# Eighteen more indirect transfers in the preparation of a four-layer graph network kernel

## The reference, cut to what matters

```python
edge_index = jnp.stack([src, dst])
x = _layernorm(x + _L0_gnn_ref(x, edge_index, ...), axis=-1)   # two GATv2 passes
x = _layernorm(x + _L1_gnn_ref(x, edge_index, ...), axis=-1)   # roles of source and target exchanged
x = _layernorm(x + _L2_gnn_ref(x, ..., edge_index), axis=-1)
x = _layernorm(x + _L3_gnn_ref(x, edge_index, ...), axis=-1)   # eight heads
```

## Time and profile before

| | us |
|---|---|
| median of 3 runs | 12944.22 |
| lowest and highest run | 12932.75 and 12955.25 |
| span of the profiled execution | 12943.7 |
| preparation, first instruction to POOL's first gather of E0 | 218.25 |
| PE busy | 10725.3 (83%) |
| POOL busy | 9352.2 (72%) |
| DVE busy | 7913.5 (61%) |

### The profile page before, as it was taken

The page is one execution under the profiler, slowest core; times in us unless marked ns, Lnnn a source line. Parts: engine busy times, 40 slices in busy tenths (PEclk is TensorE's granted clock), DMA queues, the critical chain, the costliest instruction groups (busy, mean ns, idle before and its releaser), DMA issues.

```text
span 12943.7 us, 281524 instructions
## 1 busy us (share of the span) xinstructions
PE 10725.3 (83%) x62317; PEld 8649.8 (67%) x62317; DVE 7913.5 (61%) x29130; ACT 5610.6 (43%) x14105; POOL 9352.2 (72%) x8593
## 2 busy tenths in 40 slices
PE   5788887788888878888888886999999878888886
PEld 4666666666666666666666665777777656666664
DVE  7666666666666655555555555333333568888887
ACT  1555555455555553333333335344444543333334
POOL 3777777577777758888888885777777447777775
PEclk7999999899999966666666667555555688889887
DMA  3222222422222224444444445222222222222222
GB/s 96 56 55 55 55 55 55 132 65 56 56 56 56 55 42 39 39 39 39 39 39 39 38 39 131 57 56 56 56 56 56 58 65 62 62 61 63 61 61 61
DMA packets 809108, 749.26 MB, mean 58 GB/s; under 512 B 264686, under 2 KB 691175, under 8 KB 808255
## 3 DMA queue, kind: packets, MB, share of 16 engines
q0 software_dynamic: 453440, 550.05, 24.5%
q1 hardware_dynamic: 354814, 191.38, 5.7%
HBM read 548.62 MB, written 192.13 MB: 57 GB/s over the span
## 4 chain that ended last, share of the span: by engine, by line
PE 52%; issue 9%; DVE 8%; DMA 6%; POOL 2%; ACT 2%; DVEq 2%; SPq 0%; POOLq 0%; ACTq 0%
PE bank L721 13%; PE bank L705 7%; PE bank L708 6%; DMA scatter_s<-dst_side 6%; PE bank L706 5%; PE bank L1181 4%; PE bank L1187 3%; PE bank L730 3%; PE bank L690 2%; PE bank L1196 2%; POOL scatter_s L1148 2%; DVE agg L929 1%; DVE dst_side L1274 1%; DVE lrelu L884 1%; PE bank L1190 1%
## 5 line engine op out<-in xcount | busy, mean ns | idle before, releaser
L1148 POOL DMA_INDIRECT scatter_s<-dst_side x1664 | 2566.9, 1543 | 555.4 <-DMA scatter_s<-dst_side 240.1
L808 ACT ACTIVATE oh_e<-bank,weight,minus_w 128x128 f32<-128x128 f32 x4992 | 1876.2, 456 | 1465.3 <-PE bank L730 1385.3
L920 DVE SCALAR_TENSOR_TENSOR agg<-agg,rescale,bank 128x130 f32 x4992 | 1680.8, 337 | 1211.0 <-PE bank L721 958.6
L706 PE MATMUL bank<-rows,ident 128*128 128x128 f32 x9984 | 2108.6, 296 | 0.0
L672 POOL DMA_INDIRECT rows<-gather_c,edge_sb x1664 | 1631.9, 981 | 599.6 <-issue 382.3
L672 POOL DMA_INDIRECT rows<-gather_b,edge_sb x1664 | 1605.9, 965 | 608.5 <-issue 314.8
L672 POOL DMA_INDIRECT rows<-gather_a,edge_sb x1664 | 1622.8, 975 | 555.4 <-issue 315.5
L672 POOL DMA_INDIRECT rows<-gather_s,edge_sb x1664 | 1570.3, 944 | 571.3 <-issue 378.7
L721 PE MATMUL bank<-rows,oh_e 128*128 128x130 f32 x9984 | 1873.4, 343 | 54.1 <-DVE agg L920 37.1
L721 PEld LDWEIGHTS bank<-rows,oh_e 128*128 128x128 f32 x9984 | 1601.6, 242 | 268.5 <-issue 230.4
L706 PEld LDWEIGHTS bank<-rows,ident 128*128 128x128 f32 x9984 | 1695.0, 213 | 0.0
(11 more groups left out here) (345 smaller groups left out, 19310.3 us busy)
## 6 DMA issues: line engine op xcount, KB each, us to landing
rows<-gather_a,edge_sb POOLq DMA_INDIRECT x1664
rows<-gather_b,edge_sb POOLq DMA_INDIRECT x1664
scatter_s<-dst_side POOLq DMA_INDIRECT x1664, 3.4
rows<-gather_s,edge_sb POOLq DMA_INDIRECT x1664
rows<-gather_c,edge_sb POOLq DMA_INDIRECT x1664
rows<-scatter_s SPq DMA_DIRECT2D x56, 455.0 KB, 6.1
scatter_s<-zeros SPq DMA_DIRECT2D x64, 390.0 KB, 5.7
edge_sb<-edge_tab SPq DMA_DIRECT2D x520, 40.0 KB
```

The source lines that it names most:

```text
L706: e.matmul(o, ident[:, :], rows[:, it.slot(), g, 0:P], start=False, stop=True).then_inc(L.side.sem, 1)
L808: e.activation(oh_e[:, g % 8, :], bank[7][:, (g % CH) * P:(g % CH + 1) * P], ACT.Relu, bias=weight[:, it.slot(2, 2), g:g + 1], scale=minus ...
L920: e.scalar_tensor_tensor(old, old, rescale[:, it.slot(2, 2), g:g + 1], sum_bank(g)[:, (g % 2) * AW:(g % 2) * AW + L.aw], ALU.mult, ALU.add ...
L1148: e.indirect_dma_start(scatter_s[k], bass.IndirectOffsetOnAxis(ap=S_.target[:, it.slot(1), g:g + 1], axis=0), S_.summed[:, g % 8, :], None ...
```

## The change

A column of row numbers is made, and eighteen indirect transfers are issued by POOL, three behind each of the source gathers of tiles 6 to 11, each followed by a wait for its own completion:

- behind tile 6: three gathers of 32 rows of 512 bytes from the source list into `run_max`; behind tile 7: three of 80 rows
- behind tiles 8 and 9: three scatters each of 128 rows of zeros to the spare rows of a new table, without addition, 520 bytes wide behind tile 8 and 512 bytes behind tile 9
- behind tiles 10 and 11: the same with addition, 520 and then 512 bytes wide.

POOL waits once more for all of them at the end of its preparation. On DVE a copy of `dump_row` into the first column of `cin` is put ahead of the first operation on the loaded numbers, and with it the wait for the six constants. Two tables of 12672 rows are new in device memory. Nothing reads what the new transfers write.

```diff
@@ -190,6 +190,7 @@
     res = [dram(f"residual{n}", (NB * P, P)) for n in range(2)]
+    trial = [dram(f"trial_table{n}", (NB * P + P, w)) for n, w in enumerate((XW, P))]
@@ -303,6 +304,8 @@
         ones_in_rows = counts.sem("ones_in_onehot_rows")
+        trial_rows, trial_done = counts.sem("trial_rows_made"), counts.sem("trial_transfer_done")
+        trial_at = cin[:, 0:1].bitcast(I32)
@@ -395,6 +398,23 @@
+            def trials(k):
+                e.wait_ge(trial_rows, 1)
+                for _ in range(3):
+                    if k < 2:
+                        n = (32, 80)[k]
+                        e.indirect_dma_start(run_max[0:n, :].bitcast(I32), None, a["src"],
+                                             bass.IndirectOffsetOnAxis(ap=tcoli[0:n, 0:1], axis=0)).then_inc(trial_done, 16)
+                    else:
+                        table, width = trial[k % 2], (XW, P)[k % 2]
+                        if k < 4:
+                            e.indirect_dma_start(table, bass.IndirectOffsetOnAxis(ap=trial_at, axis=0), zeros[:, 0:width], None
+                                                 ).then_inc(trial_done, 16)
+                        else:
+                            e.indirect_dma_start(table, bass.IndirectOffsetOnAxis(ap=trial_at, axis=0), zeros[:, 0:width], None,
+                                                 compute_op=ALU.add).then_inc(trial_done, 16)
+                    e.wait_ge(trial_done, 16 * (3 * k + _ + 1))
+
@@ -402,6 +422,9 @@
             for c in range(2, SC):
                 sources(c)
+                if 6 <= c < 12:
+                    trials(c - 6)
+            e.wait_ge(trial_done, 16 * 3 * 6)
@@ -442,6 +465,9 @@
             own.did(e.memset(minus_half[:, :], -0.5))
+            e.wait_ge(consts_in, 16 * 6)
+            w.wait_ge(own.so_far())
+            e.tensor_copy(trial_at, dump_row[:, :]).then_inc(trial_rows, 1)
             fb = pool_rows[:, 64:64 + SC]
```

## The result

The changed kernel takes 12983.76 us (median of 10 runs, 12969.47 to 12996.69), the kernel before 12945.47 us in the runs beside it (10 runs, 12932.75 to 12963.76). The ratio is 1.0029, with a 95% interval of 1.0020 to 1.0039: slower by 38 us, and outside the range of 12922 to 12972 us. The profiled execution of the change, with a span of 12967.7 us, is the fastest of its ten, 24.0 us over the span of before. So 14 of the 38 us of the median are not in this trace.

What follows compares the result with a forecast made beforehand. DVE was taken to bound the preparation up to E0's first gather at 218.25 us, with PE mostly in the chain behind; 0 + 1.2 + 0.4 + 0 = 1.6 us on 12944.22 gave 12945.8 us, range 12922 to 12972 us.

Steps and rivals of the forecast that it cites:

- part 4: Whole kernel: two semaphores, two unread tables and DMA time of 18 small transfers, priced at nothing.
- Part 1: Preparation, tiles 6 to 12: transfers fill POOL's idle time; tile 12's source gather at 172.1 us, cost to the path nothing.
- The bound of 179.8 us: Tile 12: latest start of POOL's source gather that still lands before DVE reads the sources at 182.36 us.
- the cover: Tiles 8 to 12: 57.1 us for four source gathers and twelve scatters before DVE waits; gone at a 4.34 us round trip.
- Part 2: Preparation: issuing eighteen transfers on POOL slows DVE's operations beside them by 1.2 us, between nothing and 1.8 us.
- Part 3: Start of DVE's work: the column copy and earlier wait for constants delay it by 0.4 us, between nothing and 0.7 us.
- The sum: Whole kernel: 0 + 1.2 + 0.4 + 0 = 1.6 us slower, all of it in the preparation.
- The rest of the kernel shifts: Rival, behind the preparation: tables, descriptor count or longer program change each turn; some 12998 or 12894 us, chance 0.03 each side.
- Slow scatters: Rival, tiles 8 to 12: scatters landing in 8.2 us delay tile 12's source gather; 12996 us, chance 0.03, smaller exposure 0.04.
- POOL holds DVE: Rival, preparation: each POOL issue stops DVE for its whole length, 24.1 us in all; 12968.7 us, chance 0.04.

Runs made afterwards that it cites:

- E0: Not a run: the kernel's stage from POOL's first gather of E0 to that of E1; 2231.2 us before, 2226.9 us in the change.
- the sixteen fills: Kernel before plus sixteen one-column fills on DVE at the place of its copy, no wait moved, TensorE at lower clock: +16 and +24 us (1.0010, 1.0018).
- the two fills: Kernel before plus two one-column fills on DVE at the place of its copy, no wait moved, at lower clock: +8, +6 and -16 us.

## Why the prediction was wrong

**What bounds the kernel.** The step that failed is the one from "nothing is added behind 218 us" to "nothing changes behind 218 us": part 4 priced the rest at nothing, and 22.8 of the trace's 24.0 us lie there. It rested on this: I took the passes for PE's, because the chain gave PE 52%, and then asked only whether the preparation ends later. The page before showed POOL's groups, with more than half of the idle time of E0's and E1's gathers ended by "issue", and the earlier trace rows showed 0.30 us between two gathers that wait for nothing. Taken together they make POOL the pace of E0, E1 and the sources: 1664 times 1.25 or 1.85 us. A busy share of 72% hid it, since the pauses are not counted as busy. With that in hand, a nanosecond on each transfer of a stage is 1.7 us, and "the rest of the kernel" can't be priced at nothing. How much it would be no row of the trace before could have told: that the issues themselves get longer was seen only afterwards.

**Part 1, the place of the transfers**: right in outcome, too short in size. Landings of the scatters were 3.7 us in the median and up to 6.0 us; the source gather of tile 12 left at 178.61 us in place of 172.1 us, and DVE did not wait. The bound of 179.8 us was nearly reached, and that DVE did not wait was partly luck. From tile 10's source gather, which DVE released at 148.00 us, two source gathers and six scatters with addition took 30.6 us, a round trip of (30.6 - 2 x 1.24) / 6 = 4.7 us in place of 3.7, and more than the 4.34 us at which the prediction had the cover gone; the plain scatters ahead of them, with 2.3 to 4.4 us to landing, were quick enough for POOL to wait for DVE once more at 148.00 us. In three of the four threes of scatters the first was the longest (tile 10: 6.25 us from its start to the next, against 3.8 us for the second).

**Part 2, POOL's issues on DVE**: right in size. L545 of tile 12 starts at 183.79 us, 1.43 us after its place before; I had 1.2 us, between nothing and 1.8. Tile 12 by itself can't show it, since the traces without any transfer differ by 1.3 us there. From tile 5 to tile 12, the stretch with the transfers beside it, DVE's rows take 81.7 us in the change and 80.1 to 80.4 us in the five traces without transfers; that is the delay. Of the 1.4 us, 0.1 us had come by tile 7, behind the gathers, which I had at 0.4 us.

**Part 3, the head**: I had 0.4 us, it was nothing. The constants landed by 5.73 us, before L450 (L476 here) was let go at the end of POOL's fill, and the copy was not held by the fill as I had assumed: it ran beside it, and the next operation starts at 7.73 us in both traces (timeline of DVE after):

```profile
5.73 0.15 DVE L470 CAST cin<-dump_row 128x1 int32<-128x1 f32 x1 [3.88 <-DMA dump_row<-in_c_dump_dram]
5.80 1.90 DVE L476 TENSOR_SCALAR rows<-rows 128x13 int32<-128x13 int32 x1
7.73 0.17 DVE L478 CAST rows<-rows 128x13 f32<-128x13 int32 x1
```

**The sum** for the preparation was 1.6 us and came out at 1.2 us. The start of E0 lies between 216.5 and 218.6 us in the five traces without transfers and the two with gathers alone, so that the close agreement is in part luck.

**Part 4, the rest**, priced at nothing, is where the cost lies. By the runs: DVE's copy and wait 19 us (alone, 1.0007 to 1.0025, so 9 to 32 us), the longer scatters 12 us (7 ns x 1664, gone without transfers), the preparation 1.2 us: 32 us of the 38, with the interval of the change from 26 to 50 us. That the parts add up is not shown: no kernel had the transfers without DVE's copy at this clock, and the change's own trace has 13.5 us in the stage of the sources but only 2.7 us in E0 and E1 together.

**The rivals.** "The rest of the kernel shifts" was the right one, with a chance of 0.03 and a mechanism that was too vague: I named tables, which cost nothing, and a count of descriptors and a longer program, which the runs bear out in part. "No row shows such a dependence" was no reason against it; the rows showed what would pass it on. "Slow scatters" and "POOL holds DVE" did not come about. In the passes it looks to be the other way round: the gathers whose issue is long have DVE's long operations beside them. Of the 24.1 us that the hold would have cost DVE, its rows of tiles 5 to 12 show some 1.4 us. The chance of 0.91 for a time within 0.2% rested on the local sum alone.

**Open.** Why two more instructions ahead of DVE's loops move the collisions into one group of the turn; that it is the length of the program and not the copy or the wait is suggested by the sixteen fills and not shown. The wait for the constants and the copy were never run apart from each other, nor the two fills where POOL sets the pace. What state makes the scatters longer. And whether the whole change with DVE's program left alone is only 12 us slower where POOL sets the pace: its three sets ran at the lower clock. Why the whole change's trace has so little of its cost in E0 and E1.

## What to carry to other kernels

Before pricing an edit at its own place, ask what passes small differences on: count the instructions of the engine that issues back to back and multiply the length of one plus the pause behind it by their number; if that is the stage's length, that engine is the bound, whatever its busy share says. In this kernel, with its thousands of equal instructions, an edit far ahead (one copy with its wait, or other forms of transfer) was worth 0.1 to 0.3% with no row of its own; for one like it the range has to hold that. Take such an edit apart by what surrounds it (tables, semaphores, one copy), not only by what it is named for.

## What was not expected of the hardware

- The time that POOL takes to issue a 520-byte scatter with addition depended on which transfers ran 4500 us before: 1542.6 ns in the mean after none or after six 128-row gathers, 1545.6 after six gathers of 32 and 80 rows, 1547.8 after six plain scatters, 1549.6 after six with addition or after all eighteen (1548 and 1550 in turns), and 1543 and 1556 in turns after three of 520 bytes. Traces of one kernel differed by about 1 ns.
- A gather of 32 or 80 rows took POOL 0.87 to 0.90 us, one of 128 rows 0.94 us; a plain scatter 0.97 to 1.09 us, one with addition 1.55 to 1.63 us.
- Beside DVE's 512-column operations a gather's issue in E1 took as much as 1.75 us in place of 0.94 us, while eighteen issues delayed DVE's own small operations by about 1.4 us in all.
- DVE's copy of one column (0.15 us, at 5.73 us) ran beside POOL's fill, which lasted until about 7.7 us, while the next operation, L476, ended only with the fill at 7.70 us.
